# A graph-attention layer over a sparse 4096 x 4096 matrix: the third quarter's shared gathers, the order of the last quarter and the place of the verdict

## The reference

```python
h = jnp.maximum(_layernorm(x), 0.0)               # x: 4096 x 128
x = x + gat(h, adj, W, a)                         # adj: 4096 x 4096 of 0.0 and 1.0, sparse
h = jnp.maximum(_layernorm(x), 0.0)
x = x + jnp.where(adj < 1, sens(adj), 0.0) @ (h @ W1 + B)

def gat(h, adj, W, a):
    Wh = h @ W
    e = leaky_relu((Wh @ a[:128])[:, None] + (Wh @ a[128:])[None, :], 0.2)
    e = where((adj > 0) | eye, e, -9e15)
    return softmax(e, axis=1) @ Wh
# sens(r) = exp(-(1/r - 1)^2 / (2 * 0.25)), which is 0 at r = 0
```

## Time and profile before

| | us |
|---|---|
| median of three runs | 218.68 (217.98 to 219.15) |
| the profiled execution | 218.19 |
| its span, first to last instruction | 216.40 |
| around the span | 1.79 |
| busy: ACT, DVE, PE, POOL | 188.0, 181.7, 153.7, 131.3 |
| moved by DMA | 76.81 MB, 355 GB/s over the span |

### The profile page before, as it was taken

How to read it: one execution, slowest core, us unless ns; L and a number is a source line. 1 busy time by engine, 2 the same in 40 slices (tenths; PEclk the granted TensorE clock), 3 DMA queues, 4 the chain that set the end, 5 groups by cost and what they waited for, 6 DMA issues and landing times.

```text
span 216.4 us, 3219 instructions
## 1 busy us (share of the span) xinstructions
PE 153.7 (71%) x956; PEld 105.3 (49%) x970; DVE 181.7 (84%) x534; ACT 188.0 (87%) x201; POOL 131.3 (61%) x141
## 2 busy tenths in 40 slices
PE   0188779982874994979929995697565977796651
PEld 0077565440452771548615762475331645575640
DVE  7993999999879899999588978995984799869772
ACT  0699987599899999999999999899999894999910
POOL 3980002294000588978877979788787888276460
PEclk9999999998599599699996999999887999999985
DMA  5999999999999999999999999999999999953012
GB/s 152 359 410 412 410 408 407 409 403 414 420 412 412 412 393 401 389 403 391 404 386 385 394 402 393 402 389 402 389 387 391 386 402 390 409 199 124 22 54 67
DMA packets 22259, 76.81 MB, mean 355 GB/s; under 512 B 2527, under 2 KB 3126, under 8 KB 22240
## 3 DMA queue, kind: packets, MB, share of 16 engines
q1 hardware_dynamic: 18912, 71.31, 84.4%
q0 software_dynamic: 2912, 5.22, 7.0%
q10 hardware_dynamic: 416, 0.07, 0.2%
HBM read 74.06 MB, written 4.23 MB: 362 GB/s over the span
## 4 chain that ended last, share of the span: by engine, by line
ACT 30%; DMA 26%; DVE 18%; PE 15%; issue 9%; POOL 0%; DVEq 0%; POOLq 0%; ACTq 0%; SPq 0%
DMA adj_ring<-in_adj 24%; ACT trash_a L943 12%; ACT trash_a L948 10%; PE bank L637 8%; DVE summed L1116 6%; ACT spread L912 3%; DVE x_sb L1439 2%; PE bank L764 1%; PE bank L624 1%; DMA gathered_rows<-node_table,shared_index 1%; DVE stats L1096 1%; DVE cand L1154 1%; ACT own_w L967 1%; PE bank L749 1%; PE bank L756 1%
## 5 line engine op out<-in xcount | busy, mean ns | idle before, releaser
L521 POOL DMA_INDIRECT gathered_rows<-node_table,index x48 | 74.2, 1546 | 38.5 <-DVE index L1290 24.5
L943 ACT ACTIVATE trash_a<-adj_ring,below_one 128x4096 fp8e4<-128x4096 f32 x19 | 70.4, 3706 | 5.4 <-DMA adj_ring<-in_adj 4.8
L637 PE MATMUL bank<-adj_ring,pack_w 128*128 128x512 bf16 (+3 forms) x255 | 69.5, 400 | 2.0 <-DMA adj_ring<-in_adj 1.0
L948 ACT ACTIVATE trash_a<-adj_ring 128x4096 fp8e4<-128x4096 f32 x19 | 68.7, 3617 | 0.6
L1116 DVE SCALAR_TENSOR_TENSOR summed<-adj_ring 128x4096 fp8e4<-128x4096 f32 x13 | 57.7, 4440 | 3.4 <-DMA adj_ring<-in_adj 3.3
L637 PEld LDWEIGHTS bank<-adj_ring,pack_w 128*128 128x128 bf16 x262 | 26.2, 104 | 30.7 <-issue 8.0
L521 POOL DMA_INDIRECT gathered_rows<-node_table,shared_index x24 | 33.0, 1376 | 10.2 <-issue 6.7
L1154 DVE MAX8 cand<-bank 128x8 f32<-128x120 f32 (+25 forms) x82 | 23.3, 351 | 3.3 <-PE bank L637 3.3
L764 PE MATMUL bank<-gathered_rows,spread 128*128 128x129 f32 x160 | 20.8, 282 | 3.6 <-DVE spread L1379 2.4
L764 PEld LDWEIGHTS bank<-gathered_rows,spread 128*128 128x128 f32 x160 | 19.4, 195 | 4.6 <-issue 4.2
L624 PE MATMUL bank<-codes,code_w 128*128 128x512 bf16 x25 | 11.0, 438 | 9.5 <-DMA adj_ring<-in_adj 6.3
(11 more groups left out here) (188 smaller groups left out, 251.7 us busy)
## 6 DMA issues: line engine op xcount, KB each, us to landing
adj_ring<-in_adj SPq DMA_DIRECT2D x32, 2048.0 KB, 22.9
node_table<-gathered_rows POOLq DMA_DIRECT2D x4, 520.0 KB, 8.4
x_sb<-in_x SPq DMA_DIRECT2D x8, 256.0 KB, 6.1
out<-x_sb SPq DMA_DIRECT2D x3, 512.0 KB, 14.2
gathered_rows<-node_table,index POOLq DMA_INDIRECT x48, 6.0
gathered_rows<-node_table,shared_index POOLq DMA_INDIRECT x24, 5.4
...
```

What stands on the lines that cost most here:

```text
L521: pool.indirect_dma_start(out=rows[:, g % RING_GROUPS * GE + t, :], out_offset=None, in_=table, in_offset=bass.IndirectOffsetOnAxis(ap=row ...
L637: last = nc.tensor.matmul(to[:, lo:hi], pack_w[:, k, :], ring_hi[:, i % AR, row_at + lo:row_at + hi], start=False, stop=(k == KB - 1), ski ...
L943: nc.scalar.activation(trash_a[:, :], ring[:, i % AR, :], ACT.Sign, bias=below_one[:, :], scale=-1.0, accum_out=signs[:, n:n + 1], saturat ...
L948: nc.scalar.activation(trash_a[:, :], ring[:, i % AR, :], ACT.Abs, accum_out=sizes[:, n:n + 1], saturate=False).then_inc(checked_a, 1)
```

## The change

- **Third quarter.** Its rest is shared by eight lanes instead of four, so g7 is four gathers instead of eight, its weights come from a table of their own (`r_oct2`), and its spread is two operations of 128x512 instead of one of 128x1024. The scores by quads and by pairs are made in one step early on, those by eight lanes twice.
- **Order.** DVE checks chunk 27 and no longer 28, ACT 28 and no longer 27, so DVE's late checks are of 26 and 27, in their own iterations and now at an iteration's end. weigh(6) and weigh(7), scatter(4) to scatter(7), epilogue(1), add_columns(2) and add_own(2) stand one or more chunks earlier, and epilogue(2) stands in iteration 31 and no longer behind pick(4). Within an iteration, epilogue comes before weigh.
- **Verdict.** POOL has nothing behind its last gather. The flag of the scores' range is made behind the all-reduce early on, those of ACT's first 16 checks (to chunk 28) ahead of g8's gathers, those of ACT's last three by two small operations of ACT each; DVE writes its flags straight into `bad`. `count_bad` waits for all of them, and `set_flag` counts non-zero ones.

The core of the diff:

```diff
-PIECES = [((0, 1, 2, 3), 32, 16, 32, 4), ((4, 5, 6, 7), 24, 16, 16, 4), ((8, 9, 10, 11), 24, 8, 32, 4),
+PIECES = [((0, 1, 2, 3), 32, 16, 32, 4), ((4, 5, 6, 7), 24, 16, 16, 4), ((8, 9, 10, 11), 24, 8, 32, 8),
...
-DVE_CHECKED = [0, 1, 2, 4, 6, 10, 11, 14, 18, 20, 22, 26, 28]
+DVE_CHECKED = [0, 1, 2, 4, 6, 10, 11, 14, 18, 20, 22, 26, 27]
-NFULL = 3 * len(PIECES)
+NFULL = 2 * len(PIECES)
-CHECK_LATE = {22: 22, 27: 26, 29: 28}
+NAL = 3
+NAP = NAC - NAL
+CHECK_LATE = {22: 22, 26: 26, 27: 27}
-QUAD_SCORES_AT, PAIR_SCORES_AT, OCT_SCORES_AT = 2, 4, 5
+QUAD_SCORES_AT, OCT_SCORES_AT = 2, (4, 5)
-WEIGH_AT = {13: 0, 17: 1, 18: 2, 21: 3, 25: 4, 26: 5, 28: 6}
-SCATTER_AT = {14: 0, 17: 1, 19: 2, 22: 3, 26: 4, 27: 5, 30: 6}
+WEIGH_AT = {13: 0, 17: 1, 18: 2, 21: 3, 25: 4, 26: 5, 27: 6, 29: 7}
+SCATTER_AT = {14: 0, 17: 1, 19: 2, 22: 3, 25: 4, 26: 5, 27: 6, 29: 7}
-ADD_COLUMNS_AT = {13: 0, 21: 1, 28: 2}
-EPILOGUE_AT = {20: 0, 28: 1}
+ADD_COLUMNS_AT = {13: 0, 21: 1, 27: 2}
+EPILOGUE_AT = {20: 0, 27: 1, 31: 2}
-ADD_OWN_AT = {13: 0, 21: 1, 29: 2}
+ADD_OWN_AT = {13: 0, 21: 1, 28: 2}
...
+            pool.wait_ge(end_max_set, 1)
+            nc.gpsimd.tensor_scalar(bad[:, BAD_END:BAD_END + 1], end_max[:, :], RANGE, 0.5, ALU.is_le,
+                                    ALU.is_lt).then_inc(judged, 1)
...
+            def judge_checks():
+                pool.wait_ge(checked_a, NAP)
+                nc.gpsimd.tensor_scalar(excess, sizes[:, 0:NAP], 2.0, None, ALU.mult).then_inc(judged, 1)
+                pool.wait_ge(judged, 2)
+                nc.gpsimd.tensor_tensor(excess, excess, signs[:, 0:NAP], ALU.add).then_inc(judged, 1)
+                pool.wait_ge(judged, 3)
+                nc.gpsimd.tensor_scalar(bad[:, 0:NAP], excess, float(HK * CW), 0.5, ALU.is_equal,
+                                        ALU.is_lt).then_inc(judged, 1)
+
             for g in range(GROUPS):
                 n = PIECE_OF_GROUP[g]
+                if g == FIRST_GROUP[HANDED]:
+                    judge_checks()
...
-            pool.wait_ge(end_max_set, 1)
-            nc.gpsimd.tensor_scalar(bad[:, BAD_END:BAD_END + 1], end_max[:, :], RANGE, 0.5, ALU.is_le,
-                                    ALU.is_lt).then_inc(judged, 1)
-            pool.wait_ge(checked_v, NVC)
-            nc.gpsimd.tensor_scalar(bad[:, BAD_V:BAD_V + NVC], bad_v[:, :], 0.0, 0.5, ALU.is_le,
-                                    ALU.is_lt).then_inc(judged, 1)
-            pool.wait_ge(full_seen, len(PIECES))
-            pool.wait_ge(shared_seen, len(PIECES))
-            nc.gpsimd.tensor_scalar(bad[:, BAD_FULL:BAD_FULL + NFULL], full[:, :, :].rearrange("p s n -> p (s n)"),
-                                    EDGE, 0.5, ALU.is_lt, ALU.is_lt).then_inc(judged, 1)
-            pool.wait_ge(checked_a, NAC)
-            nc.gpsimd.tensor_scalar(excess[:, :], sizes[:, :], 2.0, None, ALU.mult).then_inc(judged, 1)
-            pool.wait_ge(judged, 4)
-            nc.gpsimd.tensor_tensor(excess[:, :], excess[:, :], signs[:, :], ALU.add).then_inc(judged, 1)
-            pool.wait_ge(judged, 5)
-            nc.gpsimd.tensor_scalar(bad[:, 0:NAC], excess[:, :], float(HK * CW), 0.5, ALU.is_equal,
-                                    ALU.is_lt).then_inc(judged, 1)
...
             def count_bad():
-                pe.wait_ge(judged, JUDGED)
+                pe.wait_ge(judged, 4)
+                pe.wait_ge(checked_v, NVC)
+                pe.wait_ge(full_seen, len(PIECES))
+                pe.wait_ge(shared_seen, len(PIECES))
+                pe.wait_ge(last_judged, NAL)
...
-            scatter(7)
...
+                late = n - NAP
+                if late >= 0:
+                    nc.scalar.activation(sign_excess[:, late:late + 1], signs[:, n:n + 1], ACT.Identity,
+                                         bias=edges_less[:, :]).then_inc(sign_judged, 1)
                 nc.scalar.activation(trash_a[:, :], ring[:, i % AR, :], ACT.Abs,
                                      accum_out=sizes[:, n:n + 1], saturate=False).then_inc(checked_a, 1)
+                if late >= 0:
+                    act.wait_ge(checked_a, n + 1)
+                    act.wait_ge(sign_judged, late + 1)
+                    nc.scalar.activation(bad[:, n:n + 1], sizes[:, n:n + 1], ACT.Identity, scale=2.0,
+                                         bias=sign_excess[:, late:late + 1]).then_inc(last_judged, 1)
...
+                elif SET_LANES[PIECE_OF_GROUP[g]] == OL:
+                    for x in range(2):
+                        last = nc.vector.tensor_tensor(
+                            spread[:, g % 2, x * w * KB:(x + 1) * w * KB, :].rearrange("p e (o c) -> p e o c", o=2),
+                            oct_w[:, 0:w, :, :].rearrange("p e k (o c) -> p (e k) o c", o=1).broadcast_to(
+                                [P, w * KB, 2, OL]),
+                            quad_of_e[:, 2 * x:2 * x + 2].rearrange("p (o q c) -> p o q c", o=1, c=1).broadcast_to(
+                                [P, w * KB, 2, OL]), ALU.mult)
+                    last.then_inc(spread_set, 1)
...
             def set_flag():
                 dve.wait_ge(bad_reduced, 1)
-                nc.vector.tensor_reduce(flag[0:1, :], bank[7][0:1, 0:NBAD], AX.X, ALU.max).then_inc(flag_set, 1)
+                nc.vector.tensor_scalar(verdict[0:1, :], bank[7][0:1, 0:NBAD], 0.0, None, ALU.not_equal, ALU.add,
+                                        accum_out=flag[0:1, :]).then_inc(flag_set, 1)
...
+                for m in HUB_AT.get(i, ()):
+                    hub(m)
+                if i in EPILOGUE_AT:
+                    epilogue(EPILOGUE_AT[i])
+                if i in WEIGH_AT:
+                    weigh(WEIGH_AT[i])
                 if i in CHECK_LATE:
                     check(CHECK_LATE[i])
-                for m in HUB_AT.get(i, ()):
-                    hub(m)
-                if i in WEIGH_AT:
-                    weigh(WEIGH_AT[i])
-                if i in EPILOGUE_AT:
-                    epilogue(EPILOGUE_AT[i])
-            weigh(7)
             scan(STEPS - 1)
             pick(4)
-            epilogue(2)
```

134 lines of the change are left out of this document (74 added, 60 removed).

## The result

| | before | after |
|---|---|---|
| median of 19 runs each, us | 218.51 (217.80 to 219.26) | 217.14 (215.51 to 218.51) |
| ratio, 95% interval | | 0.9932 (0.9914 to 0.9949) |
| profiled execution, span, us | 218.19, 216.40 | 216.90, 215.1 |
| end of the last multiply into the output, us | 212.48 | 212.75 |
| end of POOL's drain, start of SP's, us | 216.1, 214.6 | 214.0, 214.9 |

The change makes the kernel 0.7% faster, 1.4 to 1.5 us where 1.8 were forecast. The profile says at once of what kind the gain is: the data end 0.27 us later than before, and still the span is 1.3 us shorter. The times of one program now lie 3 us apart, before 1.5 (up to 2.3 beside other experiments); what bears on that comes with the experiments. All ratios leave out an execution more than 1.5% above the fastest of its kernel, of which there are two, one with scatter(6) later and one with both edits.

The account below looks back on a forecast made before the run. The tail without loads bounds it, POOL ending 1.6 us behind the data. Verdict gains; the chain's 1.73 us goes largely to own_w and the clock: data 212.3, span about 214.6, -1.8 us, 216.6 against 218.4; range 214.9 to 218.7.

Parts of the forecast that it names:

- The verdict: POOL's end: six small operations leave it, so POOL no longer ends 1.6 us behind the data; most of -1.8 us.
- the two readings of the drain: POOL's drain at the end: 6.4 us after its last operation, or 8.6 us after the last gather.
- Case (b): POOL's drain counts from the last gather and g9's gathers slip up to 1.3 us: 217.9; 0.20 shared with another rival.
- the long drain: POOL's drain taken as 8.6 us after the last gather, ending at 214.4.
- DVE's walk: DVE's new order at old durations: index(3) at 189.3, scan(15) at 193.9, pick_shared(4) at 196.3 instead of 198.03.
- case (c): Moved check(26) on DVE holds g6's gathers, delaying weigh(6) and everything behind; 219.5 at 3 us; chance 0.07, half above 219.5.
- x: Delay of g6's rows beyond the walk's 174.95 for weigh(6); before is reached at 2, slower by over 0.5% from 3.
- The chain's term of 1.73 us: DVE's pick_shared(4) at 196.3 instead of 198.03 takes 1.73 us off the chain to shared_index and g9's gathers.
- own_w and the clock: ACT's own_w ends at 202.25, not 199.05, holding PE's add_own; some 3.4 us at 1.2 GHz cost 1.1 to 1.7.
- Case (a): PE's clock stays at 2.4 GHz and POOL's drain counts from its last operation: time 215.4; chance 0.17.

Follow-up runs that it names:

- scatter(6) later: Changed kernel with scatter(6) one chunk later on PE, behind pack(28) instead of ahead of it; ratio to the kernel before 0.9915 (0.9891 to 0.9939).
- both edits: Changed kernel with scatter(6) behind pack(28) and ACT's last own_w ahead of the check of chunk 30; ratio to the kernel before 0.9906 (0.9881 to 0.9931).
- PE busy: Changed kernel with matmuls that nobody reads in PE's waits of the tail; ratio to the kernel before 0.9888 (0.9867 to 0.9909).
- own_w early: Changed kernel with ACT's last own_w ahead of the check of chunk 30, not 31; ratio to the kernel before 0.9939 (0.9915 to 0.9962).

## Why the prediction was right, and where it was not

**The verdict: right, and it suffices for the gain.** The forecast was that POOL stops being last and that most of the 1.8 us is what it stood behind the data. Its drain went from 216.1 to 214.0, and the verdict alone gives 0.992. It isn't the only way: with six operations back on POOL's end the new lanes and order give 0.9928, which the prediction did not weigh. Of the two readings of the drain the first held: 6.05 us after the last operation (6.4 before), so it doesn't take the 8.6 us from the last gather. Case (b), which needed the long drain, could not occur. What it feared did happen in small: a gather of g9 that started at 205.32, within weigh(8)'s spread (204.58 to 205.81), took 1.34 us instead of 1.00.

**DVE's walk: wrong behind weigh(6).** The walk put index(3) at 189.3 and pick_shared(4) at 196.3; they came at 191.26 and 197.59. Weigh(6) was 1.1 us late (176.03 against 174.95): DVE came to the check of chunk 26 at 166.26, right behind weigh(5), where the walk has it start near 165.3, and the gather that it held ended as much later. That is case (c) with x about 1. The step that failed stands behind it: the walk takes PE's work at its old durations and looks at PE's clock in the tail only, although the new order makes PE wait for weigh(6) with scatter(6) and pack(28) behind. In the changed kernel's profile the clock fell after that wait, and from weigh(6) to index(3) it took 15.23 us where the walk has 14.35; with the clock full it took 13.86, so that the walk would have had half a microsecond to spare. The chain's term of 1.73 us was 0.33 at shared_index, and nothing at g9's gathers, since g8's were late too. With PE busy pick_shared(4) came 195.98 - 191.55 = 4.43 us behind the start of pack(31), before 198.03 - 191.88 = 6.15: 1.72 less, so the term was right in size where the clock let it through.

**own_w and the clock: right.** own_w ended at 202.93 (202.25 forecast, chunk 28 came 0.7 later), add_own was released by it, and the level fell to 1.2 GHz for 3.4 us from 202.6. The forecast gave 1.1 to 1.7 us for it; holding the clock brought 1.0. What was missing is that the fall isn't tied to this wait: with own_w early it comes over scatter(8), elsewhere over add_columns. So that it came over add_own in this profile, as forecast, is in part luck. Case (a), a full clock, gives 0.9888 with matmuls put there for it; 215.62 was measured where (a) said 215.4, in a kernel that is not the changed one.

**Sum.** Data at 212.75 (212.3 forecast), SP's drain 2.15 behind (2.1), span 215.1 (214.6), median 217.14 (216.6). The data's end came by the path that the forecast named, own_w, add_own at half the clock and the scatters; the half microsecond is chunk 28's, which came 0.7 us later than interpolated and moved own_w by as much. Index(3)'s delay isn't in it: g9's gathers were 0.23 us ahead of that path. So the chain's missing term did not show in the time, because the forecast had own_w and the clock hold the data anyway. The gain is the 1.6 us that POOL's chain stood behind the data, less the 0.27 us that the data lost.

A rule of the Trainium skill, "SBUF — State Buffer", section "Who interferes with whom", was weighed ahead: by its inference a spread can't hold a gather, and the gather of g9 that took 1.34 us speaks against it as the rows of before did. The same section says that issue order decides who blocks. The two runs with a gather 0.06 us ahead of the check (1.02 us) and 0.66 us behind its start (4.63 us) agree with that.

## What stays open

The distance of 3 us between executions of the changed kernel was not taken apart run by run. The profiles of kernels with its order differ in two things, where PE's clock falls and whether g6's last gather starts ahead of the check; with PE busy the distance is 1.5 us over six executions. Why the clock falls behind some waits and not behind others of the same length stays open as well. A version in which the check can't hold that gather wasn't tried. What eight lanes alone bring, without the verdict, wasn't either, and which of lanes and order lets six operations on POOL's end go free was not separated.
